# Moving one DRAM write of an attention kernel from SyncE's queue to GpSimd's

## The reference

```
Q, K, V = x @ Wq.T, x @ Wk.T, x @ Wv.T          # split into 16 heads of 16
idx    = clip(k - q, -256, 256) + 256            # distance of key k from query q
scores = (Q . K + Q . pek[idx]) / 4              # causal: k <= q only
attn   = softmax(scores)
out    = attn . V + attn . pev[idx]              # then @ Wo.T
```

## Time and profile before

| | |
|---|---|
| median of 3 runs | 6529.61 us (6526.24 to 6539.48) |
| the profiled execution: time, span | 6522.48 us, 6520.8 us |
| busy: TensorE, its weight loads | 5398.4 us (83%), 3549.1 us (54%) |
| busy: VectorE, ScalarE, GpSimd | 3837.4 us (59%), 3448.9 us (53%), 1941.0 us (30%) |
| mean granted clock of TensorE | 0.924 |
| HBM read, written | 775 MB, 705 MB |

### The profile page before, as it was taken

One profiled execution on the slowest core, in us unless ns is written; L12 is line 12 of the kernel. 1 busy time (PEld: TensorE's weight loads), 2 busy tenths in 40 slices (PEclk: granted clock), 3 DMA queues, 4 the chain that ended last, 5 costly groups with the idle time before them and its releaser, 6 DMA issues. The chain is left out here.

```text
span 6520.8 us, 161883 instructions
## 1 busy us (share of the span) xinstructions
PE 5398.4 (83%) x49460; PEld 3549.1 (54%) x49460; DVE 3837.4 (59%) x8681; ACT 3448.9 (53%) x7512; POOL 1941.0 (30%) x2580
## 2 busy tenths in 40 slices
PE   9968888788788878877888878778778799999998
PEld 5645555555555555555555555555555455555555
DVE  5656666666666666666656666566666544444444
ACT  4547666666666666666666666666666511111111
POOL 4443333333333333333333333333333211111111
PEclk9989999898999899998989999899989899999999
DMA  8989888888888888888988888888889611111111
GB/s 247 284 238 293 279 279 280 267 277 278 273 277 279 271 281 278 281 277 265 280 276 283 280 275 277 270 284 277 275 263 290 232 40 50 51 51 51 51 51 36
DMA packets 694617, 1491.84 MB, mean 229 GB/s; under 512 B 68132, under 2 KB 365704, under 8 KB 693640
## 3 DMA queue, kind: packets, MB, share of 16 engines
q1 hardware_dynamic: 693640, 1480.16, 72.2%
HBM read 775.21 MB, written 704.65 MB: 227 GB/s over the span
## 5 line engine op out<-in xcount | busy, mean ns | idle before, releaser
L741 ACT ACTIVATE a_prob<-a_neg_s,a_neg_max 128x384 f32<-128x384 f32 (+2 forms) x2048 | 1172.5, 573 | 316.8 <-issue 155.5
L472 DVE COPY a_p_t<-a_t_ps 128x512 f32<-128x512 f32 (+3 forms) x1536 | 954.3, 621 | 341.5 <-PE a_t_ps L705 336.4
L638 PE MATMUL a_s_ps<-a_k,a_q 96*128 96x512 bf16 (+3 forms) x3072 | 910.6, 352 | 274.7 <-issue 139.5
L712 PE MATMUL a_t_ps<-a_ident,a_band 128*128 128x128 f32 x3840 | 668.0, 297 | 567.2 <-DMA a_band<-prob_scr 540.3
L748 ACT ACTIVATE a_b_out<-a_t_ps 128x512 f32<-128x512 f32 (+1 forms) x1024 | 580.8, 567 | 1021.0 <-PE a_t_ps L648 1013.1
L705 PE MATMUL a_t_ps<-a_ident,a_prob 128*128 128x128 f32 x5376 | 959.1, 280 | 0.4 <-DVE a_band_t L478 0.2
L784 DVE TENSOR_REDUCE a_far_neg<-a_s_ps 128x1 f32<-128x640 f32 (+4 forms) x1280 | 710.4, 555 | 415.1 <-PE a_s_ps L638 367.2
L790 DVE CUSTOM_DVE_ANT_1 a_neg_s<-a_s_ps,a_bias,a_far_neg 128x384 f32<-128x384 f32 x1280 | 790.5, 618 | 241.1 <-DVE a_far_neg L784 241.1
L666 PE MATMUL a_o_ps<-a_p_t,a_v 128*32 128x128 f32 x18432 | 890.6, 307 | 47.1 <-issue 46.9
L712 PEld LDWEIGHTS a_t_ps<-a_ident,a_band 128*128 128x128 f32 x3840 | 453.3, 150 | 720.1 <-DMA a_band<-prob_scr 359.4
L748 ACT ACTIVATE a_p_t<-a_t_ps 128x512 f32<-128x512 f32 (+3 forms) x1536 | 667.3, 434 | 154.4 <-PE a_t_ps L705 149.5
(11 more groups left out here) (97 smaller groups left out, 6658.2 us busy)
## 6 DMA issues: line engine op xcount, KB each, us to landing
a_bias<-bias_scr SPq DMA_DIRECT2D x512, 576.0 KB, 5.5
bias_scr<-a_b_out SPq DMA_DIRECT2D x512, 512.0 KB, 6.5
a_band<-prob_scr SPq DMA_DIRECT2D x512, 512.0 KB, 6.2
prob_scr<-a_prob SPq DMA_DIRECT2D x448, 576.0 KB, 7.1
qk_scr<-p_parts SPq DMA_DIRECT2D x128, 384.0 KB, 3.3
a_q<-qk_scr SPq DMA_DIRECT2D x384, 128.0 KB, 5.1
a_k<-qk_scr SPq DMA_DIRECT2D x384, 128.0 KB, 5.7
prob_scr<-a_wide SPq DMA_DIRECT2D x64, 576.0 KB, 5.7
```

The lines of the kernel that those rows point to most:

```text
L472: copy(p_t[par][:, u, blocks[0] * P:(blocks[-1] + 1) * P], bank[:, 0:len(blocks) * P]) \
L638: mm = pe.matmul(s_ps[:, u % 2, c:e], q_s[0:ROWS, g, u, qb * P:(qb + 1) * P], k_s[0:ROWS, g, u, c:e], start=True, stop=True)
L712: mm = pe.transpose(bank[:, n * P:(n + 1) * P], band[:, kk % 2, 2 * i + n // 2, (n % 2) * P:(n % 2 + 1) * P], ident[:, :])
L741: e = act.activation(near_prob(k, u, near(qb)), neg_s[:, u % 2, 0:w].rearrange("p (b c) -> p b c", c=P), ACT.Exp, bias=neg_max[:, u:u + 1] ...
```

## The change

The write of the widened probabilities is no longer in SyncE's list. GpSimd starts it at the end of `widen`, in its own queue. Two waits come before it there: for its own addition (`wide_ready`, T + 1) and for the slot's last reader (`r_mm` of tile k-4). The transfer, its slots and its semaphore `p_saved` stay as they are.

```diff
--- before.py
+++ after.py
@@ -525,10 +525,6 @@
                         sp.wait_ge(p_saved[(k - 2) % 4], quad(r, k - 2))
                         src = bass.AP(prob_scr.tensor, (k - 2) % 4 * P * WIDE + 1, [[WIDE + 1, P], [1, ROW]])
                         sp.dma_start(band[:, par].rearrange("p h j -> p (h j)"), src).then_inc(p_loaded[par], 16)
-                    if k >= 0 and ok(k - 1):
-                        sp.wait_ge(wide_ready, T)
-                        rows = prob_scr[(k - 1) % 4].rearrange("(q c) -> q c", c=WIDE)
-                        sp.dma_start(rows, wide_prob(k - 1)).then_inc(p_saved[(k - 1) % 4], 16)
                     if k + 2 >= 0 and ok(k + 2):
 
                         par, slot = k % 2, (k + 2) % 4
@@ -600,6 +596,11 @@
                 pool.tensor_tensor(slots(p if qb else wide0, X_RAW if qb else 0, GRP + 1),
                                    (older if qb >= 2 else none)[:, :, :],
                                    slots(p, X_OWN - MAXD, GRP + 1), ALU.add).then_inc(wide_ready, 1)
+                pool.wait_ge(wide_ready, T + 1)
+                if valid(k - 4, first, last):
+                    pool.wait_ge(r_mm, 2 * (T - 4) + 2)
+                pool.sem_inc(pool_turn, 1)
+                pool.dma_start(prob_scr[k % 4].rearrange("(q c) -> q c", c=WIDE), wide_prob(k)).then_inc(p_saved[k % 4], 16)
 
             def mask(r, k):
```

## The result

The changed kernel takes 6667.76 us (median of 4 runs, 6652.93 to 6691.3), the kernel before 6527.92 us (4 runs). The ratio is 1.0214, 95% interval 1.0182 to 1.0247: 2.1% slower. The forecast was 6720 us. The profiled execution of the changed kernel is the slowest of its four (6691.3 us, span 6689.6), so its excess over the profiled execution of before is 169 us, where the medians say 140.

A forecast was written before the change was run, and what follows sets the result against it. The attention stage was taken to be bound by TensorE's waits for a late a_band, through a DRAM chain. 480 us more less 255, half carried (112), plus 79 of slow clock, made 191 and 6720 us; range 6312 to 6912.

The forecast's parts named there:

- GpSimd's issue: At the end of `widen`: 0.8 us from the addition's end until the write is queued, covered by GpSimd's idle time.
- The stall that goes: In SyncE's queue: all 255 us of waiting at the band load for the write to land would go.
- The band load: In the DMA engines: the write takes 1.42 us from the band load at 338 places, 480 us more wait of TensorE.
- How much carries to the end: In TensorE's band waits: of 225 us net added, half carries to the end, 112 us.
- The clock: On TensorE: 0.7 us of slow clock for each carried microsecond of wait, 79 us.
- Masks, bias load, and the added wait for the slot's reader: On GpSimd and in SyncE's queue: masks covered by idle time, bias write and load cancel, reader's wait; all counted at nothing.
- Rival A: In the write-to-band-load chain: the band load isn't held up and 255 us go, 6312 us, faster; chance 0.32.
- C: At GpSimd's issue: it takes the whole lead, both chains stay, 6530 us; chance 0.12 together with a late GpSimd write.
- B: In the attention stage: TensorE's delay passes on each time, 382 us, 6912 us, slower still; chance 0.14.

The follow-up runs named there:

- 8 KB run: The kernel before, plus a write of 8 KB by GpSimd in each tile, SyncE's list untouched: ratio 1.0015.
- the old order: The changed kernel, with GpSimd also waiting for SyncE's issue of the band load of the tile before, ahead of the write: ratio 1.0135 over the kernel before.
- ScalarE's run: Against the kernel before, the write of the widened probabilities leaves SyncE's list and ScalarE issues it in its own queue, nothing by GpSimd: ratio 1.0186.
- the early loads: The kernel before with the q, k and v loads issued ahead of SyncE's wait for the bias load: ratio 0.9505.
- four lists: The change on the kernel before (1.0214), with q, k, v loads early (5.1% slower), bias write early too (4.6% slower), later-round q, k, v loads left out (1.011).

## Why the prediction was right

Sign, size and range held: 6668 against 6720, in 6312 to 6912. By its own steps:

- **GpSimd's issue**: 0.8 us from the addition to the start was predicted, 0.69 measured on average, 0.57 long. The forward move of the write, 1.4 us less this, was to be 0.6 us and was 0.86 (1.55 to 0.69); that three tiles gave a fair mean was luck, for the median of all 512 is 0.85. Its cost of nothing is confirmed by the 8 KB run (1.0015).
- **The stall that goes**: I let all 255 us go. 95 went and 160 stayed. This step failed: I took the write's landing for queueing that it would be rid of, "under 6 us". It stayed at 6.9. That this is because it shares the engines is my reading; from ScalarE's queue it was 5.6. What was gained is nearly only the earlier start.
- **The band load**: predicted 1.42 us later at 338 places, 480 us. Measured 0.8 us later at the median. 1.42 was the case of the whole write going ahead everywhere; it was started ahead in 28% of the tiles. At 338 places 0.8 us would be 270 us, so the loss was put some 210 us too high and the gain above 160 too high. The mechanism is thus shown in part only: with the old order in two queues most of the loss stayed.
- **How much carries to the end**: the net was to be 225 us of wait, half of it carried, 112. The wait rose by 67 us (540 to 607) and TensorE's idle time in the stage by 65: a net three times too large, and a halving that didn't take place. These two errors met, and 112 against 65 is what was left of them.
- **The clock**: 0.7 us for each carried microsecond of wait, 79 us, was predicted; the profiled execution has 103 us for 65, 1.6 for one, and the median execution about 76 by the estimate above, 1.2 for one. So the term came out at its size because a rate that was too low met a carried wait that was too large. No fixed rate holds: in the stage, busy against idle time of TensorE moved by 80 and 23 us in ScalarE's run, by 30 and 30 with the old order, by 136 and 201 less with the early loads. What goes with the slow clock in these rows is the number of long stops; that they are its cause no run isolates.
- **Masks, bias load, and the added wait for the slot's reader**: at nothing, as predicted. GpSimd's waits for the bias load ahead of a mask fell from 1544 us in 512 tiles to 682 us in 393, so more than half of the cover was used. The bias load landed 0.4 us earlier; the write no longer stands in front of it in the list.
- **Rival A** (the chain wins) fails on the wait and the landing; **C** on the ratio in ScalarE's queue and on the start at 0.67 us; **B** needs SyncE's wait for maxima "well over 907 us". It is 1425, and the time that SyncE no longer spends on the write explains at most 305 of the 518 us more. B's rule, that the delay passes on each time, is the one that held (65 of 67 us); its price, 6912, wasn't reached, since it rests on the same 225 us.

Shown by runs: it isn't GpSimd's path (ScalarE's queue 1.019, 8 KB 1.0015). Putting the order of the two transfers back, with a later start of the write, gives back 0.8 of the 2.1 points; leaving out the q, k and v loads takes away half. These two may overlap, so they don't add up. Still open: why a second queue with the whole write in it costs 1.1 to 1.9% with the old order (GpSimd's or ScalarE's) or with a short line. In these runs the mean time from the addition to the landed band is within 0.1 us of what it was without the change, but the long waits are more. The DMA share falls with the rate in the changed kernel, so the engines aren't busier; what makes single band loads late, no run here separates.

## What to carry to other kernels

A write that starts and lands earlier from another queue gains nothing by that alone. Here it landed 1.0 us sooner after the addition, but the band load behind it started later and took 0.7 us longer, and TensorE's waits for it became longer. Ask who waits for the transfers that are in flight with it, and what else holds up the next link. Look in one queue's own list first: put the transfers that nobody waits for soon into the time in which that queue stands waiting, ahead of the wait and not behind it. Here this was worth 7%, with every transfer in one queue, while the write in GpSimd's queue cost 1 to 5% on each of four lists.

## What the runs showed of the hardware

- Two queues: a lone transfer in the second one, GpSimd's, landed no sooner after its issue (the write 6.9 us, before 7.1; the band load 7.2, before 6.2), while from ScalarE's queue the write landed after 5.6 us. The Trainium skill ("DMA: Bandwidth & Descriptors", Queues, rings and completion order) has the engines go round robin between queues; ScalarE's 5.6 us would fit a turn of its own, but its write also starts 2.2 us later after the addition than GpSimd's (2.92 and 0.69 us), so it meets other transfers; GpSimd's 6.9 us does not show one.
- GpSimd was held by its DMA's issue for 0.57 us in nearly every case (573 to 749 ns), where SyncE's issue of the same write took 0.32 to 1.62 us.
- A mean DMA share of 0.88 at 278 GB/s was no limit: 0.93 and 308 GB/s were reached with the same transfers in another order.
- TensorE lost 1.6 us to the slow clock for each microsecond of added idle time in the profiled execution of the changed kernel (103 and 65 us), 3.5 in ScalarE's run (80 and 23), and got back 0.7 with the early loads (136 and 201). Beside it, its waits for a_band of over 2 us went from 88 to 151 and to 138 in the first two, and to 28 in the third.
